# The ternary feed-forward of one transformer layer run as half steps between the pairs of the cross-attention ahead of it

## The chip, the cores and the metric

The kernel runs on one core of one Trainium2 chip. The metric is the device time of one execution in microseconds, from the first to the last instruction with what lies around it; lower is better. Each time given for a kernel is the median of several executions, and the profile is of one execution of its own.

## The reference

Two layers on x (32 batches, 64 tokens, 256 columns) with a context of 1601 keys per batch. Cut to what matters here, in the order in which it is computed:

```
x = x + xattn0(layernorm(x), ctx)       # one head of 256, 1601 keys
x = x + attn0(layernorm(x))             # causal, 64 tokens of a batch
x = x + ffn0(layernorm(x))              # the part that the change moves
x = x + xattn1(layernorm(x), ctx)       # 16 heads
x = x + attn1(layernorm(x))
x = x + moe1(layernorm(x))              # 8 experts, two per token

def ffn0(x):
    h = bit_linear(x, w1)               # 256 -> 1024
    h = silu(depthwise_conv1d(h))       # 3 taps along the 64 tokens, bias
    return bit_linear(h, w2)            # 1024 -> 256

def bit_linear(x, w):
    scale = 127 / clip(max(abs(x), axis=-1), 1e-5)
    xq = round(x * scale) / scale       # a scale per token
    ws = 1 / clip(mean(abs(w)), 1e-5)
    wq = clip(round(w * ws), -1, 1) / ws
    return xq @ wq.T
```

## The kernel before

The kernel is written by hand in five queues (sync, gpsimd, scalar, tensor, vector); each engine runs its own list in order, and semaphores tie them together. There is no planner: the order of the work is the order of the statements.

Phase A holds the first cross-attention and the causal attention. x lies in SBUF as 16 tiles of 128 tokens (two batches each). For every tile (a "pair", `pe_pair_a`, `act_pair_a`, `vec_pair_a`) TensorE multiplies the folded queries with the two batches' contexts (line 1040, four score chunks in PSUM banks 4 to 7), VectorE takes the row maximum over 1601 columns (line 1578), ScalarE the exp (line 738), TensorE transposes the probabilities (line 1049, 13 blocks), VectorE copies them to SBUF (lines 1586 and 1588), TensorE weighs the context rows (line 1060), prepares the next tile's queries, transposes the result and applies the output matrix (line 1077). The causal attention of the tile before runs in between (`transpose_xs`, `project_s`, `scores_s`, `transpose_p_s`, `weigh_s`; `norm_s`, `mask_s`, `add_s` on VectorE). The 14 middle pairs are a hardware loop. SP loads the transposed context of the next pair when the scores are done and the rows of it when the weighted sum is done (lines 370 and 372).

Phase F, the ternary feed-forward, starts when all of x is through phase A. It runs 4 chunks of 512 tokens, one after the other. In each, VectorE normalises and quantises four tiles to bf16 integers, TensorE transposes them and multiplies with the ternary w1 (line 1117, eight blocks of 128 hidden rows), VectorE scales the result by the token's step into a padded buffer (line 1647), POOL computes the centre tap and bias (line 537), VectorE the two side taps (lines 1518 and 1520), ScalarE the silu (line 775). Then VectorE takes the maximum over all 1024 hidden rows of every token (line 1653 across the eight blocks, then over partitions through a transpose), scales (line 1670; POOL takes the odd blocks, line 542) and rounds them (line 1672), TensorE multiplies with the ternary w2 (line 1133) and VectorE adds the product to x (line 1676).

Phase B, the second cross-attention and what follows, waits for all of x (XDONE_F): SP loads w_kv then (line 391). SP's queue between the last scores and that load holds the w_cp loads, two large pad_rows stores to slots_d and a context load. Phase M, the experts, comes last.

The steps of the prediction touch the lines above, `rsqrt` on POOL (lines 495 and 497), and the reload of weights at the start (VectorE rounds w1 and w2, lines 1538 to 1542).

## Time and profile before

| | |
|---|---|
| median of 3 runs | 2910.5 us (2908.04 to 2916.0) |
| the profiled execution | 2910.0 us |
| its span | 2908.3 us |
| TensorE matmul busy | 2535.7 us (87%) |
| VectorE busy | 1727.1 us (59%) |
| ScalarE busy | 1337.5 us (46%) |
| GpSimd busy | 907.7 us (31%) |
| DMA | 283.13 MB, mean 97 GB/s |

The busy times are sums over the whole span and mix phases with different limits. In the rows further down PE is TensorE, DVE is VectorE, ACT is ScalarE, POOL is GpSimd and SPq is the queue of SyncE, from which the loads are issued. Starts are in us from the start of the span. What stands in square brackets behind a row of the timeline is how long the engine had sat idle before it, and what ended that.

### The profile page before, as it was taken

The page shows a single profiled execution, that of the slowest core. Times are in us where ns is not written, and L with a number is a line of the kernel's source. Part 1 is how long each engine was busy: PE and PEld are TensorE (multiplying, and loading weights), DVE is VectorE, ACT ScalarE, POOL GpSimd, SP SyncE. Part 2 cuts the span into 40 slices and gives each one's busy share as a digit, 9 for nine tenths or more (in the row PEclk, how much of TensorE's full clock was granted, in tenths as well). Part 3 has the DMA queues.
Part 4 walks back from the last instruction along what each step waited for, and adds up shares of the span by engine and source line. Part 5 has one row for each costly group of instructions (what it writes and reads, how often), then busy time and mean ns, then how long its engine had stood idle before and what let it go on. Part 6 is the DMA issues. An engine that isn't in the chain of part 4 may idle for free.

```text
span 2908.3 us, 76158 instructions
## 1 busy us (share of the span) xinstructions
PE 2535.7 (87%) x32240; PEld 2148.8 (74%) x32244; DVE 1727.1 (59%) x2970; ACT 1337.5 (46%) x2130; POOL 907.7 (31%) x910
## 2 busy tenths in 40 slices
PE   6999933318999999999999999999999986999997
PEld 3555511117888888888888888888888864999997
DVE  3434367752465675665665665665666664677775
ACT  1211211114555555555555555555555532555554
POOL 1000023344434434434434434434434401111111
PEclk9999956558999999999999999999999986999999
DMA  8878780001101101101101101101101010666664
GB/s 334 324 309 324 288 262 0 0 18 36 46 25 36 39 28 36 39 28 36 39 28 36 39 28 36 39 28 36 39 28 37 28 49 8 209 205 211 212 204 144
DMA packets 60985, 283.13 MB, mean 97 GB/s; under 512 B 4881, under 2 KB 35986, under 8 KB 46098
## 3 DMA queue, kind: packets, MB, share of 16 engines
q1 hardware_dynamic: 52562, 268.73, 25.6%
q0 software_dynamic: 8160, 10.29, 2.2%
q8 instruction: 238, 3.90, 0.5%
q14 instruction: 25, 0.20, 0.0%
HBM read 247.45 MB, written 33.65 MB: 97 GB/s over the span
## 4 chain that ended last, share of the span: by engine, by line
issue 37%; PE 27%; POOL 21%; DVE 7%; DMA 5%; ACT 3%; POOLq 1%; SPq 0%; ACTq 0%; DVEq 0%
POOL k_lo L561 7%; POOL ctx_lo L569 6%; PE PS L1060 3%; PE PS L1040 3%; PE PS L1428 2%; PE PS L1429 2%; PE PS L1430 2%; POOL qbd_lo L574 2%; DMA unit_raw<-in_experts 2%; PE PS L1352 1%; DMA sum_d<-scaled,xg 1%; PE PS L1188 1%; POOL sideB L588 1%; PE PS L1176 1%; DVE mpart L1696 1%
## 5 line engine op out<-in xcount | busy, mean ns | idle before, releaser
L1696 DVE TENSOR_REDUCE mpart<-PS 128x1 f32<-128x802 f32 (+1 forms) x512 | 484.8, 985 | 254.8 <-PE PS L1176 253.3
L869 ACT ACTIVATE probs<-PS 128x1024 f32<-128x1024 f32 (+1 forms) x416 | 413.4, 1025 | 218.6 <-PE PS L1352 218.6
L569 POOL TENSOR_TENSOR ctx_lo<-ctx_raw,ctx_hi 128x801 fp32r<-128x801 f32 x128 | 223.4, 1756 | 360.8 <-ACT ctx_hi L804 352.3
L561 POOL TENSOR_TENSOR k_lo<-probs,k_hi 128x400 fp32r<-128x400 f32 (+1 forms) x256 | 248.9, 972 | 262.8 <-ACT k_hi L792 262.8
L1352 PE MATMUL PS<-qbd_hi,k_hi 64*128 64x256 f32 (+1 forms) x1664 | 314.0, 374 | 0.0
L1176 PE MATMUL PS<-k_hi,qbd_hi 128*128 128x512 f32 (+2 forms) x1024 | 266.2, 361 | 28.6 <-POOL ctx_lo L569 14.1
L791 ACT COPY probs<-PS 128x400 f32<-128x400 f32 (+1 forms) x256 | 126.3, 493 | 243.0 <-PE PS L1156 213.5
L1163 PE MATMUL PS<-wkv_hi,ctx_hi 128*128 128x256 f32 (+1 forms) x832 | 236.5, 284 | 0.0
L1188 PE MATMUL PS<-probs,vals 128*32 128x64 f32 x13312 | 234.7, 221 | 2.0 <-issue 1.8
L1352 PE MATMUL PS<-qbd_hi,k_lo 64*128 64x256 f32 (+1 forms) x1664 | 235.3, 279 | 0.5 <-issue 0.4
L1352 PE MATMUL PS<-qbd_lo,k_hi 64*128 64x256 f32 (+1 forms) x1664 | 234.7, 279 | 0.0
L1165 PE MATMUL PS<-wkv_hi,ctx_lo 128*128 128x256 f32 (+1 forms) x832 | 234.3, 282 | 0.0
L1164 PE MATMUL PS<-wkv_lo,ctx_hi 128*128 128x256 f32 (+1 forms) x832 | 233.5, 281 | 0.0
L1188 PEld LDWEIGHTS PS<-probs,vals 128*32 128x32 f32 x13312 | 197.3, 110 | 42.4 <-issue 25.1
L1176 PEld LDWEIGHTS PS<-k_hi,qbd_hi 128*128 128x128 f32 x1024 | 175.7, 192 | 62.7 <-DVE mpart L1696 41.0
L1428 PE MATMUL PS<-xT_hi,unit_hi 128*128 128x256 f32 x736 | 209.2, 284 | 3.2 <-DVE xT_lo L1936 2.9
L794 ACT COPY vals<-PS 128x512 f32<-128x512 f32 x192 | 112.8, 588 | 214.8 <-PE PS L1165 214.8
L1429 PE MATMUL PS<-xT_lo,unit_hi 128*128 128x256 f32 x736 | 208.9, 284 | 0.0
L1430 PE MATMUL PS<-xT_hi,unit_lo 128*128 128x256 f32 x736 | 208.7, 284 | 0.0
L1154 PE MATMUL PS<-ctx_hi,wkv_hi 128*128 128x400 f32 (+1 forms) x512 | 187.2, 366 | 17.9 <-POOL ctx_lo L569 17.9
L675 POOL DMA_INDIRECT sum_d<-scaled,xg x46 | 75.6, 1643 | 350.7 <-DVE scaled L1967 343.7
L1155 PE MATMUL PS<-ctx_lo,wkv_hi 128*128 128x400 f32 (+1 forms) x512 | 178.6, 349 | 0.0
(321 smaller groups left out, 6229.6 us busy)
## 6 DMA issues: line engine op xcount, KB each, us to landing
unit_raw<-in_experts SPq DMA_DIRECT2D x46, 1536.0 KB, 6.9
ctxN<-in_ctxN SPq DMA_DIRECT2D x16, 3328.0 KB, 10.7
ctxT<-in_ctxT SPq DMA_DIRECT2D x16, 3204.0 KB, 10.5
ctx_raw<-in_ctxT SPq DMA_DIRECT2D x64, 801.0 KB, 4.5
slots_d<-pad_rows SPq DMA_DIRECT2D x2, 9360.0 KB, 44.8
xg<-slots_d SPq DMA_DIRECT2D x23, 260.0 KB, 2.7
x<-in_x SPq DMA_DIRECT2D x1, 2048.0 KB, 9.8
sum_d<-x SPq DMA_DIRECT2D x1, 2048.0 KB, 13.7
```

The source lines that it names most:

```text
L561: g.tensor_tensor(k_lo[:, n, a, c:c + width], k_raw[p % 2][:, 0:width], k_hi[:, n, a, c:c + width].bitcast(F32), ALU.subtract).then_inc(s. ...
L569: g.tensor_tensor(ctx_lo[:, a, cols], ctx_raw[:, cols], ctx_hi[:, a, cols].bitcast(F32), ALU.subtract).then_inc(s.ctx_lo_ready, 1)
L869: act.activation(probs[rows, t % PROBS, :], PS[rows, 1024 * (t % 2):1024 * (t % 2) + 1024], ACT.Exp).then_inc(s.pr_ready, 1)
L1163: pe.matmul(to, ctx_hi[:, k, keys], wkv_hi[:, k, D:2 * D], start=k == 0, stop=False)
L1165: mm = pe.matmul(to, ctx_lo[:, k, keys], wkv_hi[:, k, D:2 * D], start=False, stop=k == KT - 1)
L1176: mm = pe.matmul(at, qbd_hi[:, n, pair // 4, (pair % 4) * P:(pair % 4) * P + P], k_hi[:, n, pair // 4, c:c + width], start=True, stop=True)
L1188: mm = pe.matmul(bank(4, S, slice(32 * j, 32 * j + 32), g * S), vals[rows, n, mine:mine + 32], probs[rows, t % PROBS, at_head(h):at_head(h ...
L1352: mm = pe.matmul(bank(2 * (t % 2) + r, 256, rows, a * 256), keys_part[part, n, a, keys], queries[part, n, a, r * 256:r * 256 + 256], start ...
L1428: pe.matmul(to, hi[:, k, cols], tokens_hi[:, k, :], start=k == 0, stop=False)
L1429: pe.matmul(to, hi[:, k, cols], tokens_lo[:, k, :], start=False, stop=False)
L1430: mm = pe.matmul(to, lo[:, k, cols], tokens_hi[:, k, :], start=False, stop=k == KT - 1)
L1696: v.tensor_reduce(mpart[:, pair, half:half + 1], PS[:, at:at + width], AX, ALU.max).then_inc(s.mx_red, 1)
```

## The change

Phase F as a stage of its own goes. Its work is cut into 8 chunks of 256 tokens, and each chunk into tasks at fixed distances (3 to 18) from its first half step 4f. Half step 2i runs inside pair i of phase A, half step 2i+1 between pairs i and i+1; steps 33 to 46 come after the last pair. Every queue is written out (the loop over pairs too) and calls the tasks by `chunk_at`. POOL keeps the reciprocal roots only: ScalarE computes the centre tap from PSUM, with 1x256 per block, and VectorE both side taps from PSUM. VectorE alone multiplies all 2048 hidden columns of a chunk by the row scale and rounds them, in two instructions. The step of x is multiplied in before the first product instead of after it, so that product runs on float32r in two parts (high and rest), with w1 kept as float32r. Silu is one instruction of 2048 columns, with a dummy exp behind it while phase A lasts. ScalarE takes two of the four copies of the transposed probabilities. The causal attention uses banks 0 and 2, the output product bank 7, and banks 1 and 3 belong to the feed-forward. The last score chunk waits for the normalised tile (`xs_ready`).

The diff, cut to its core:

```diff
-CHUNK = 512
+CHUNK = 256
+HID_BUFS = 3
+GROUPS = HT // 2
+FFN_STEPS = 4 * CHUNKS + 15
+def chunk_at(step, at):
+    f, late = divmod(step - at, 4)
+    return [f] if late == 0 and 0 <= f < CHUNKS else []
-        w1q = sb("w1q", [P, KT, HID], BF16)
+        w1q = sb("w1q", [P, KT, HID], F32R)
 # gpsimd
+            def ffn(at):
+                for _ in chunk_at(at, 3) + chunk_at(at, 5):
+                    rsqrt(mv_f, rstd_f)
...
 # scalar
+            def centre_taps(q):
+                f, m = divmod(q, GROUPS)
+                act.wait_ge(s.h_ps, q + 1)
+                for n in range(2):
+                    j = 2 * m + n
+                    act.activation(hidden_f[:, f % HID_BUFS, j, :], bank(1, CHUNK, at=n * CHUNK), ACT.Identity,
+                                   bias=convb[:, j:j + 1], scale=convw[:, j, 1:2]).then_inc(s.h_mid, 1)
+            def ffn(step):
+                for m in range(GROUPS):
+                    for f in chunk_at(step, 9 + m):
+                        centre_taps(GROUPS * f + m)
+                for f in chunk_at(step, 8):
+                    act.wait_ge(s.xf_ps, f + 1)
+                    act.copy(xsT_hi[:, :, :].rearrange("p k t -> p (k t)"), bank(3)).then_inc(s.xf_hi_ready, 1)
+                for f in chunk_at(step, 17):
+                    act.wait_ge(s.rows_ps, f + 1)
+                    act.copy(rowscale[:, :], bank(3, CHUNK)).then_inc(s.rows_ready, 1)
+                for f in chunk_at(step, 13):
+                    act.wait_ge(s.taps_done, HT * (f + 1))
+                    mine = hidden_f[:, f % HID_BUFS, :, :].rearrange("p j t -> p (j t)")
+                    act.activation(mine, mine, ACT.Silu).then_inc(s.silu_done, 1)
+                    if step < 2 * TILES:
+                        act.activation(reload[:, :], eps[:, :], ACT.Exp)
             # act_pair_a, after the exp and copy_qkv
+                act.wait_ge(s.pT_ps, 4 * i + 2)
+                act.copy(probsAT[:, 4:8, :].rearrange("p t q -> p (t q)"), bank(6)).then_inc(s.pTa_ready, 1)
+                act.wait_ge(s.pT_ps, 4 * i + 4)
+                act.copy(probsAT[0:LAST_KEYS, 12, :], bank(0, P, slice(0, LAST_KEYS))).then_inc(s.pTa_ready, 1)
+                ffn(2 * i)
...
             # its end, after the copy of attT
+                ffn(2 * i + 1)
 # tensor
+            def hidden_group(q):
+                f, m = divmod(q, GROUPS)
+                if q:
+                    pe.wait_ge(s.taps_done, 2 * q)
+                if m == 0:
+                    pe.wait_ge(s.xf_lo_ready, f + 1)
+                for n in range(2):
+                    cols = slice((2 * m + n) * P, (2 * m + n) * P + P)
+                    for a in range(KT):
+                        pe.matmul(bank(1, CHUNK, at=n * CHUNK), w1q[:, a, cols], xsT_hi[:, a, :], start=a == 0, stop=False)
+                        mm = pe.matmul(bank(1, CHUNK, at=n * CHUNK), w1q[:, a, cols], xsT_lo[:, a, :], start=False, stop=a == KT - 1)
+                mm.then_inc(s.h_ps, 1)
+            # ffn(step): groups at 9 to 12, transposes of x at 8, of the maxima at 15,
+            # row scales at 17, second product (16 matmuls) at 18
             # pe_pair_a
                 if not first:
                     transpose_xs()
                     project_s()
+                ffn(2 * i)
                 pe.wait_ge(s.probsA_ready, T["probsA"].up())
...
                 if not first:
                     weigh_s()
+                ffn(2 * i + 1)
                 pe.wait_ge(s.attT_ready, T["attT"].up())
 # vector
+            def side_taps(q):
+                f, m = divmod(q, GROUPS)
+                v.wait_ge(s.h_mid, 2 * (q + 1))
+                # for both blocks the left tap, then for both the right one:
+                    v.scalar_tensor_tensor(acc[:, :, 1:S], h[:, :, 0:S - 1], convw[:, j, 0:1], acc[:, :, 1:S], ALU.mult, ALU.add)\
+                     .then_inc(s.vec_step, 1)
+                v.wait_ge(s.vec_step, T["step"].up(2))
...
+            def hidden_max(f, k):
+                v.wait_ge(s.silu_done, f + 1)
+                v.tensor_reduce(hmax[:, k * P:k * P + P], hidden_f[:, f % HID_BUFS, :, k * P:k * P + P].rearrange("p j t -> p t j"), AX, ALU.max,
+                                apply_absolute_value=True).then_inc(s.hmax_ready, 1)
+            def scale_hidden(f):
+                mine = hidden_f[:, f % HID_BUFS, :, :]
+                v.wait_ge(s.rows_ready, f + 1)
+                stepped(v.tensor_tensor(mine, mine, rowscale[:, None, :].broadcast_to([P, HT, CHUNK]), ALU.mult))
+                v.tensor_scalar(hq[:, :, :], mine, MAGIC, MAGIC, ALU.add, ALU.subtract).then_inc(s.hq_ready, 1)
+            def ffn(step):
+                for f in chunk_at(step, 8):
+                    rest_of_xf(f)
+                for m in range(GROUPS):
+                    for f in chunk_at(step, 9 + m):
+                        side_taps(GROUPS * f + m)
+                for f in chunk_at(step, 17):
+                    scale_hidden(f)
+                for f in chunk_at(step, 18):
+                    add_ffn(f)
+                for f in chunk_at(step, 15):
+                    hidden_steps(f)
+                for k in range(TPC):
+                    for f in chunk_at(step, 3 + 2 * k):
+                        moments_f(TPC * f + k)
+                    for f in chunk_at(step, 13 + k):
+                        hidden_max(f, k)
+                for k in range(TPC):
+                    for f in chunk_at(step, 4 + 2 * k):
+                        quantise_x(TPC * f + k)
             # vec_pair_a
                 if not first:
                     norm_s(x[:, i - 1, :])
+                    ffn(2 * i - 1)
                 v.wait_ge(s.scores_ps, T["scores"].up())
...
                 if not first:
                     mask_s()
+                ffn(2 * i)
                 v.wait_ge(s.probsA_ready, T["probsA"].up())
```

`rest_of_xf` subtracts the high part of the transposed x from PSUM (512 columns). `quantise_x` normalises a tile, takes its row maximum, and scales, rounds and rescales it: four instructions on 256 columns and five on one. `hidden_steps` reduces the transposed maxima (256 columns), has four small instructions and two diagonals of 128 columns. `add_ffn` adds two tiles.

## Rows read from the trace of the kernel before

**Rows 1.** Windows: start:end, us, busy of PE, PEld, DVE, ACT, POOL, clock, DMA, GB/s.
```profile
26.00:366.00 340.00, 306.12 (x2083) 181.95 (x2083) 140.24 (x363) 66.21 (x169) 22.14 (x60) 0.99 0.80 313
378.00:625.00 247.00, 73.66 (x300) 39.39 (x304) 186.20 (x336) 38.99 (x63) 83.70 (x88) 0.57 0.18 57
```

**Rows 2.** Timeline of PE over one pair: start, duration, instruction, count, idle before.
```profile
219.49 5.61 PE L1040 MATMUL PS<-ctxT,big 128*64 128x512 f32 x32
...
226.94 1.13 PE L1016 MATMUL PS<-w_sv,big 128*128 128x256 f32 x4
228.93 1.64 PE L1049 MATMUL PS<-ident,big 128*128 128x128 f32 x13 [0.86 <-ACT big L738]
...
240.53 0.65 PE L1040 MATMUL PS<-ctxT,big 128*64 128x512 f32 x2
```

**Rows 3.** Timeline of DVE over the same pair.
```profile
219.71 0.42 DVE L1599 TENSOR_TENSOR x<-PS,x 128x256 f32 x1 [0.77 <-PE PS L1077]
...
221.97 0.41 DVE L1494 TENSOR_SCALAR big<-x,mv_s,rstd_s 128x256 f32 x1 [0.93 <-POOL rstd_s L497]
225.14 1.82 DVE L1578 TENSOR_REDUCE small<-PS 128x1 f32<-128x1601 f32 x1 [2.77 <-PE PS L1040]
...
229.62 1.89 DVE L1586 COPY big<-PS 128x512 f32<-128x512 f32 x3 [0.46 <-PE PS L1049]
...
236.87 0.48 DVE L1595 TENSOR_SCALAR cat<-PS,small 128x256 f32<-128x256 f32 x1 [4.39 <-PE PS L1060]
...
239.49 0.48 DVE L1570 SCALAR_TENSOR_TENSOR x<-PS,small,x 128x256 f32 x1 [2.08 <-PE PS L1029]
```

**Rows 4.** Timeline of ACT over the same pair.
```profile
225.50 0.37 ACT L718 COPY big<-PS 128x256 f32<-128x256 f32 x1 [7.12 <-PE PS L1006]
227.19 1.60 ACT L738 ACTIVATE big<-PS,small 128x1601 f32<-128x1601 f32 x1 [1.32 <-DVE small L1580]
```

**Rows 5.** Timeline of PE at the end of phase A.
```profile
364.56 1.13 PE L1077 MATMUL PS<-vout,attn_ch 128*128 128x256 f32 x4
368.35 0.44 PE L1006 MATMUL PS<-ident,big 128*128 128x128 f32 x2 [2.66 <-DVE big L1494]
...
370.48 2.07 PE L1016 MATMUL PS<-w_sv,big 128*128 128x256 f32 x4
```

**Rows 6.** Timeline of SP's queue after the last scores.
```profile
351.38 7.97 SPq L377 DMA_DIRECT2D w_cp<-in_w_cp  x16
...
384.66 28.16 SPq L388 DMA_DIRECT2D ctx_raw<-in_ctxT  x1
625.11 0.36 SPq L391 DMA_DIRECT2D probs<-in_w_kv  x1
```

**Rows 7.** Lines by form, one chunk of phase F: busy us, mean ns, then idle before.
```profile
L1653 DVE TENSOR_REDUCE big<-ctxN 128x512 f32<-128x4096 f32 x1 | 7.2, 7171 | 0.7 <-ACT ctxN L775 0.7
...
L1627 DVE TENSOR_REDUCE small<-big 128x1 f32<-128x256 f32 x4 | 1.4, 408 | 0.0
...
L1629 DVE TENSOR_SCALAR small<-small 128x4 f32<-128x4 f32 x1 | 0.2, 169 | 0.0
```

**Rows 8.** Timeline and source of long DVE rows outside phase F.
```profile
634.04 1.22 DVE L1866 TENSOR_TENSOR wkv_lo<-probs,wkv_hi 128x1024 fp32r<-128x1024 f32 x1 [0.97 <-ACT wkv_hi L882]
...
L1542 DVE TENSOR_SCALAR w1q<-work x1: 1227/1227/1227, 29.0 to 29.0; 128x2048 bf16<-128x2048 f32 x1
```

**Rows 9.** Lines by form, ACT in the same chunk of phase F.
```profile
L775 ACT ACTIVATE ctxN<-work 128x512 f32<-128x512 f32 x8 | 5.0, 629 | 13.1 <-DVE work L1520 13.1
...
L775 ACT ACT_TABLE_LOAD x1 | 1.3, 1283 | 0.0
```

**Rows 10.** Timeline of PE, 52 f32r matmuls; the first and the last.
```profile
666.39 0.28 PE L1164 MATMUL PS<-wkv_lo,ctx_hi 128*128 128x256 f32 x1
...
672.41 0.28 PE L1164 MATMUL PS<-wkv_lo,ctx_hi 128*128 128x256 f32 x1
```

**Rows 11.** The chain that ended last, first pair: transposes of the probabilities.
```profile
37.88 3.04 PE PS L1049 x13
```

More of the change, by code:

```diff
@@ L1027, in weigh_s, with added @@
             def weigh_s():
                 pe.wait_ge(s.spT_ready, T["spT"].up())
-                pe.matmul(bank(2, D, at=256), pT_s, v_s, start=True, stop=True).then_inc(s.so_ps, 1)
+                pe.matmul(bank(2, D), pT_s, v_s, start=True, stop=True).then_inc(s.so_ps, 1)
                 T["x_done"].up()
-            def pe_pair_a(first, last):
+            def added(f):
+                return min(2 * (2 * f + 8) + 1, 2 * TILES) + TPC * (f + 1)
+            def hidden_group(q):
[10 more added lines that the diff above has]
+                mm.then_inc(s.h_ps, 1)
@@ L1035, in pe_pair_a @@
+            def pe_pair_a(i):
+                first, last = i == 0, i == TILES - 1
                 pe.wait_ge(s.qk_ready, T["qk"].up())
@@ L1037, in pe_pair_a @@
                 for n, (c, width) in enumerate(KEY_CHUNKS):
+                    if n == len(KEY_CHUNKS) - 1 and not first:
+                        pe.wait_ge(s.xs_ready, i)
                     for k in range(KT):
@@ L1557, in mask_s @@
                 v.wait_ge(s.ss_ps, T["ss"].up())
-                v.tensor_tensor(s_s, bank(3, P), causal[:, :], ALU.add).then_inc(s.vec_step, 1)
+                v.tensor_tensor(s_s, bank(2, P, at=256), causal[:, :], ALU.add).then_inc(s.vec_step, 1)
                 v.wait_ge(s.vec_step, own())
@@ L1569, in add_s, with stepped @@
                 v.wait_ge(s.so_ps, T["so"].up())
-                v.scalar_tensor_tensor(xi, bank(2, D, at=256), small[:, 7:8], xi, ALU.mult, ALU.add).then_inc(s.x_done, 1)
+                v.scalar_tensor_tensor(xi, bank(2, D), small[:, 7:8], xi, ALU.mult, ALU.add).then_inc(s.x_done, 1)
                 T["x_done"].up()
-            def vec_pair_a(before, xi, after):
-                if before is not None:
-                    norm_s(before)
+            def stepped(ins):
+                ins.then_inc(s.vec_step, 1)
+                v.wait_ge(s.vec_step, own())
@@ new lines, in scale_hidden, with add_ffn @@
+            def scale_hidden(f):
[3 more added lines that the diff above has]
+                v.tensor_scalar(hq[:, :, :], mine, MAGIC, MAGIC, ALU.add, ALU.subtract).then_inc(s.hq_ready, 1)
+            def add_ffn(f):
+                v.wait_ge(s.o_ps, f + 1)
+                for k in range(TPC):
+                    xk = x[:, TPC * f + k, :]
+                    v.scalar_tensor_tensor(xk, bank(3, D, at=k * D), h_step[:, k:k + 1], xk, ALU.mult, ALU.add).then_inc(s.x_done, 1)
+                T["x_done"].up(TPC)
@@ L1595, in vec_pair_a @@
                 v.tensor_scalar(att, bank(4, D), small[:, 3:4], None, ALU.mult).then_inc(s.att_ready, 1)
[L1596 to L1597 removed]
+                if not first:
+                    add_s(x[:, i - 1, :])
                 v.wait_ge(s.outA_ps, T["outA"].up())
[L1599 removed]
+                v.tensor_tensor(xi, bank(7, D), xi, ALU.add).then_inc(s.x_done, 1)
                 T["x_done"].up()
[L1602 removed]
+            vec_pair_a(0)
@@ L1603, in _ @@
             v.wait_ge(s.weights_in, WEIGHTS_IN)
-            with v.Fori(1, TILES - 1) as i:
-                enter("A", i, 1)
-                vec_pair_a(tile_of_x(i - 1), tile_of_x(i), tile_of_x(i + 1))
-            leave("A", TILES - 2, 1)
-            vec_pair_a(x[:, TILES - 2, :], x[:, TILES - 1, :], None)
+            for i in range(1, TILES):
+                vec_pair_a(i)
             norm_s(x[:, TILES - 1, :])
+            ffn(2 * TILES - 1)
             mask_s()
+            ffn(2 * TILES)
@@ L1679, in _, with tile_of_x @@
-            leave("F", CHUNKS)
+            for step in range(2 * TILES + 1, FFN_STEPS):
+                ffn(step)
+            v.wait_ge(s.x_done, XDONE_F)
+            def tile_of_x(i):
+                return x[:, bass.ds(i, 1), :].rearrange("p a n -> p (a n)")
             def end_batch(b):
```

367 lines of the change are left out of this document (141 added, 226 removed).

## The prediction

> **What bounds the kernel now.** I read the windows by stage first. [rows 1] give two stages before the second cross-attention: the first cross-attention (26 to 366 us), TensorE busy 306 of 340 us at clock 0.99, and the ternary feed-forward (378 to 625 us), TensorE busy 74 of 247 us, VectorE 186, clock 0.57. The change folds the second stage into the first, so I then read one pair of the first engine by engine. One pair takes 21.04 us from scores to scores [rows 2]. TensorE hardly pauses: its largest wait is the 0.86 us for the softmax. VectorE in the same pair [rows 3] waits 2.77 us for the scores and 4.39 us for the weighted sum; ScalarE waits 7.12 us in one piece [rows 4]. So the pair is TensorE's, and the others have holes in two places: at the seam between pairs, and in the middle behind the softmax.
>
> In [rows 5] stands the last pair: its output matmul ends at 364.56 + 1.13 = 365.69. [rows 6] have SP issuing the w_kv load at 625.11, as soon as the last feed-forward tile is added. These **259.4 us** are what the change replaces; the 2283 us after it run the same code and I leave them as they are. The profiled execution took 2910.0 us (span 2908.3 and 1.7 around it), the median of the runs is 2910.5, so nothing has to be converted. A difference of 0.3% (9 us) is about what a measurement of this kernel can tell.
>
> **The prices of a half step, on VectorE.** A chunk is now 256 tokens (8 chunks) and its work is spread over half steps 4f+3 to 4f+18. Per chunk:
> - taps of one hidden group: four scalar_tensor_tensor on 252 PSUM columns, the 256-column one is 0.48 and overlaps its follower slightly [rows 3]: 1.8 us, four times. The centre tap moves from POOL to ScalarE (two copies' worth of 0.37 [rows 4]).
> - scale and round, 2048 columns: the 1024-column tensor_tensor takes 1.22, so 2048 take 1.22 + 1024 x 1.04 ns = 2.3; the rounding to bf16 of 2048 columns is 1.23 [rows 8]. Together 3.55.
> - maximum over the hidden rows: 7.17 us for 4096 read across rows [rows 7], a quarter each: 1.8, twice. At the rate of the plain reduce of 1601 in 1.82 [rows 3] it would be 1.2.
> - quantise a tile: four operations on 256 columns at up to 0.41 [rows 3, 7], four small ones at 0.17: 2.3, twice. Moments: between the add (ends 220.13) and the wait for POOL (from 221.04) [rows 3]: 0.9, twice.
> - maxima to steps: 0.41, four small ones, two 128-column diagonals at about 0.25: 1.7. Rest of x: a 512-column read of PSUM, 0.7. Adding two tiles: 0.9.
>
> With every fourth half step the same four kinds recur: seam A (steps 17, 9, 13, 5 of four chunks) 1.8 + 3.55 + 1.8 + 0.9 = 8.05; middle A 1.8 + 0.9 + 1.8 + 2.3 = 6.8; seam B 1.8 + 1.7 + 0.9 = 4.4; middle B 0.7 + 1.8 + 2.3 = 4.8. That is 24 us a chunk.
>
> **On TensorE.** f32r matmuls of 256 columns follow each other every (672.41 - 666.39) / 51 = 0.118 us [rows 10]. A hidden group is 8 of them, 1.1 us with its tail; the second product is 16 of bf16, put at the same rate, 1.9; the transposes of x 0.6, those of the maxima 0.44, the row scales 0.55 (a 128-column f32 transpose is 1.64 / 13 [rows 2], a matmul with its diagonal twice that).
>
> **What of it lies on the path.** Two stretches of a pair.
> - From the first score matmul to the first probability transpose: 9.4 us now [rows 2]. VectorE's lane in it: normalised 2.9 us after the start (222.38), then the half step, then maximum, negation and exp, 225.14 to 228.93 = 3.8 [rows 2, 3]. With seam B 2.9 + 4.4 + 3.8 = 11.1, **+1.7**; with seam A 14.75, **+5.3**. TensorE's own lane is 8.6 (end of the v projection, 228.07) plus 1.7 or 3.0 of the middle half step: 10.3 and 11.6, hidden under VectorE's. TensorE then pauses some 3 us for the softmax after seam A.
> - From there to the end of the output matmul: 11.6 us. VectorE has 4.39 of waiting, some 0.9 from two of four copies of the probabilities (three take 1.89 [rows 3], the last is short) that ScalarE takes, and about 1.2 more, since TensorE takes att only after the next queries: 6.5. Middle B (4.8) costs nothing; middle A (6.8) **+0.4**. TensorE does seam work ahead of the output matmul, 1.65 or 1.55, less 0.25 of a wait it covers: **+1.4 and +1.3**. Were this cover gone, 4.8 and 6.8 would come on top in full.
>
> ScalarE: at seam A it has two centre taps, a copy, a table load of 1.28, silu on 2048 columns (512 take 0.63 [rows 9], and 1601 take 1.60 [rows 4], so about 2.0) and the load back with a dummy exp, 1.5: 5.9 us in its hole of 7.12. Off the path; in the middle it has 2 us in 4 of idle time.
>
> Two pairs: 1.7 + 5.3 + 0.4 + 1.4 + 1.3 = 10.1 us, so 26.1 a pair. The pipeline fills slowly: laid out with the same lanes, pairs 1 to 3 cost nothing, the next four 1.1, 1.6, 2.2 and 3.0, then four times 10.1, and the last pair 1.5 more, since it loses a shortening that TensorE had without next queries. **Stage one grows by 7.9 + 40.4 + 1.5 = 50 us.**
>
> **The tail**, half steps 31 to 46 on VectorE after the last output matmul: 4.4 + 4.8 + 8.05 + 6.8 + 3.5 + 2.5 + 7.15 + 4.5 + 3.5 + 1.8 + 5.35 + 2.7 + 1.7 + 0 + 3.55 + 0.9 = 61.2, with 3.1 for the last tile of the causal attention: 64.3. Its waits, as TensorE at the lower clock (0.57 in this stage now [rows 1]; 2.07 / 1.13 times longer [rows 5], with its fixed part a little more) needs 2.1 for a group and 3.6 for the second product: 1.8 around that tile, 2.3 for the transposed x, 4.2 for hidden groups, 5.7 for three second products, 0.9 and 1.6 for maxima and row scales: 16.5. **81 us**.
>
> Added waits: the last score chunk waits for the normalised tile (ready 2.9 us in, wanted after about 5.1), a hidden group for the taps of the one before, always a half step old until the tail; neither holds what is queued behind it. The loop over pairs is written out; the last pair, written out already, shows no issue waits [rows 5], so I cost it at nothing. SP's queue isn't late: from the last scores, w_cp and pads take 384.66 - 351.38 = 33.3 and the ctx_raw issue 28.2 [rows 6], 61 us, and w_kv is asked for at about 104. The context loads of a pair have more time than now. POOL keeps two small operations per tile; its memset after the stage stays behind the same signal.
>
> **Sum:** 2910.0 - 259.4 + 50 + 81 = **2782 us** (2781.6).
>
> **The clock, by row and by rule.** After the pause of 2.66 us and thin work, the v projection ran 2.07 us where a matmul group of the same count and width took 1.13 [rows 5]; 13 transposes at the start took 3.04 [rows 11] against 1.64 [rows 2]. A dense stretch like the pair before such a pause is nowhere in the trace, so a pause of 3 us costs between nothing and a lower clock on the transposes (1.4 us as at the start) and some of the weighted sum behind them, 2 us in all. I take nothing, as work before and behind the pause is dense. The Trainium skill (TensorE: Matmul & The Clock Gate, section HAM oscillation) says that a kernel whose TensorE keeps pausing between short bursts loses its clock at each pause; by it the sum would be 4 x 2 = 8 us more.
>
> **Bounds.** Low: maxima at 1.2, taps 1.5, scaling 3.3, quantise 2.0, TensorE at 2.4 GHz: stage one +38, tail 64, 2910.0 - 259.4 + 102 = 2753. High: groups at 1.9 (lower clock everywhere), scaling 4.6, taps 2.0, quantise 2.8: +73 and 100, 2824.
>
> **Rivals.**
> 1. The pauses of seam A cost the clock each time: four times 2, **2790**. For it: [rows 5]. Against: a burst of over 20 us precedes. Chance 0.17.
> 2. Nothing overlaps, since each queue runs in its order and VectorE's half steps hold up the maximum and att in full: the whole 24 us a chunk lands in the path, stage one +131 (24 x 8 = 192 less the tail's 61) in place of 50: **2863**. The change then doesn't do what it says. Against: the holes of [rows 3]. Chance 0.06.
> 3. Slower than before: once the weave is full (eight pairs), the pauses keep TensorE at 1.2 GHz between them. A pair has 306.12 / 340 x 21.04 = 18.9 us of TensorE work [rows 1] and half of a chunk's 7.9, 22.9; at half clock it costs 22.9 less some 2.7 of pauses, 20.2 more, eight times 162: **2944**. It decides from 128 / 20.2 = 6.3 such pairs on. Against: clock 0.99 with 90% busy [rows 1]; the new busy share is 22.9 / 26.1 = 88%. For it: nothing but the 0.57 of the thin stage. Chance 0.03.
>
> **Numbers.** Forecast 0.74 with its own range 2753 to 2815, rivals 0.17, 0.06, 0.03. The range 2753 to 2824 holds the first two cases nearly whole and leaves out a little over 0.1. Faster by over 0.3%: 0.74 + 0.17 + 0.06 = 0.97, less 0.01 for a mix of rivals 2 and 3 near zero: 0.96; same 0.01; slower 0.03.
>
> **What would show it.** In the profile after: pairs alternating near 24.2 and 28.2 us between output matmuls, with VectorE never waiting for the scores at seam A; TensorE waiting about 3 us for the softmax every second pair at clock 1.0; the last output matmul near 416 us, the w_kv issue near 497; silu of 2048 columns near 2.0 and two table loads a chunk up to chunk 4. Wrong if pairs are even at 21 to 22 (ScalarE and VectorE cheaper), if the clock is below 0.9 in stage one, or if the tail is over 100 us.

## The result, and the profile after it

The changed kernel takes **2774.5 us** (median of 4 runs, 2772.3 to 2778.8) beside 2910.4 us for the kernel before: ratio **0.9532**, 95% interval 0.9514 to 0.9550, so 136 us or 4.7% less. A second set of five runs gave 2774.1 us beside 2907.8, ratio 0.9536 (0.9523 to 0.9550). The forecast was 2782.

The profiled execution took 2772.3 us, its span is 2770.6. TensorE was busy for 91% of it, VectorE 61%, ScalarE 50%, GpSimd 30%. The windows by stage, as in [rows 1], with the same columns; the second stage is now only the tail of the woven feed-forward, from the last output matmul to the w_kv load:

```profile
26.00:406.00 380.00, 343.53 (x2387) 221.52 (x2387) 244.87 (x646) 128.11 (x277) 32.47 (x88) 0.97 0.74 287
406.00:484.00 78.00, 39.80 (x188) 29.05 (x186) 59.68 (x127) 20.54 (x36) 2.21 (x6) 0.69 0.66 202
```

TensorE works in 90% of the first stage, as before, and VectorE in 64% where it was 41%. The timeline of PE, then that of SP's queue, at the end of the stage answer to [rows 5, 6]:

```profile
405.46 1.03 PE L1141 MATMUL PS<-vout,attn_ch 128*128 128x256 f32 x4
```

```profile
384.73 7.30 SPq L388 DMA_DIRECT2D w_cp<-in_w_cp  x16
...
417.90 28.20 SPq L399 DMA_DIRECT2D ctx_raw<-in_ctxT  x1
484.42 0.36 SPq L402 DMA_DIRECT2D probs<-in_w_kv  x1
```

The last output matmul ends at 406.49 (365.69 before: +40.8) and w_kv is issued at 484.42 (625.11 before). So the replaced 259.4 us became 40.8 + 77.9 = **118.7 us**, where the forecast had 50 + 81 = 131. What follows w_kv takes 2770.6 - 484.4 = 2286.2 us, 3.0 more than before the change; in a second trace of the changed kernel it takes 2281.5, 1.7 less than before the change, so the rest is unchanged within what one execution varies. SP is through with its stores and the context load at 446.1, 38 us before w_kv is asked for. For this reason the issue of w_kv is the measure in the experiments below: it leaves out the noise of 2280 us of unchanged code.

The timeline of PE in a long and a short pair, beside [rows 2]:

```profile
226.18 5.61 PE L1098 MATMUL PS<-ctxT,big 128*64 128x512 f32 x32
...
235.55 1.92 PE L1084 MATMUL PS<-w2q,hq 128*128 128x256 bf16 x16
240.20 2.38 PE L1110 MATMUL PS<-ident,big 128*128 128x128 f32 x13 [2.73 <-ACT big L752]
...
243.23 6.36 PE L1123 MATMUL PS<-ctxN,big 128*64 128x256 f32 x52
...
254.20 2.37 PE L1098 MATMUL PS<-ctxT,big 128*64 128x512 f32 x10
...
264.49 1.64 PE L1110 MATMUL PS<-ident,big 128*128 128x128 f32 x13 [0.32 <-ACT big L752]
266.48 5.83 PE L1123 MATMUL PS<-ctxN,big 128*64 128x256 f32 x52
...
277.15 5.60 PE L1098 MATMUL PS<-ctxT,big 128*64 128x512 f32 x32
```

The pairs alternate as forecast: 28.02 us (226.18 to 254.20) and 22.95 (to 277.15), 28.2 and 24.2 expected. The long one pauses 2.73 us for the softmax. What was not in the sum stands right behind the pause: 13 transposes take 2.38 instead of 1.64, and the weighted sum 6.36 instead of 5.83. From the first transpose to the end of the sum it is 243.23 + 6.36 - 240.20 = 9.39 us, in the short pair 7.82. Windows of that stretch, in the columns of [rows 1], have TensorE's granted clock (third number from the end) at its upper level through the pause, lower behind it, and up again before the pair is over:

```profile
237.00:240.00 3.00, 0.47 (x5) 0.17 (x2) 2.00 (x6) 1.54 (x2) 1.16 (x3) 1.00 1.01 424
240.20:244.30 4.10, 4.10 (x21) 3.17 (x23) 2.46 (x7) 2.36 (x7) 0.00 (x0) 0.59 0.30 125
247.00:250.00 3.00, 3.00 (x28) 1.72 (x23) 2.83 (x8) 0.00 (x0) 0.00 (x0) 1.00 0.00 0
```

VectorE at the seam of that long pair, and its second maximum, beside [rows 3]:

```profile
228.44 0.41 DVE L1520 TENSOR_SCALAR big<-x,mv_s,rstd_s 128x256 f32<-128x256 f32 x1 [0.93 <-POOL rstd_s L508]
228.77 0.86 DVE L1613 SCALAR_TENSOR_TENSOR hidden_f<-PS,convw,hidden_f 128x252 f32<-128x252 f32 x2
229.66 0.87 DVE L1619 SCALAR_TENSOR_TENSOR hidden_f<-PS,convw,hidden_f 128x252 f32<-128x252 f32 x2
230.45 2.28 DVE L1645 TENSOR_TENSOR hidden_f<-hidden_f,rowscale 128x2048 f32<-128x2048 f32 x1
232.76 1.23 DVE L1646 TENSOR_SCALAR hq<-hidden_f 128x2048 bf16<-128x2048 f32 x1
233.91 1.95 DVE L1625 TENSOR_REDUCE hmax<-hidden_f 128x128 f32<-128x1024 f32 x1
...
236.45 1.79 DVE L1685 TENSOR_REDUCE small<-PS 128x1 f32<-128x1601 f32 x1
...
246.52 1.93 DVE L1625 TENSOR_REDUCE hmax<-hidden_f 128x128 f32<-128x1024 f32 x1
```

The 2.77 us wait for the scores of [rows 3] is gone: from 228.44 on VectorE runs without a gap up to the maximum over 1601 columns. ScalarE in the same seam, beside [rows 4, 9]:

```profile
226.28 1.28 ACT L743 ACT_TABLE_LOAD   x1
227.57 1.91 ACT L743 ACTIVATE hidden_f<-hidden_f 128x2048 f32<-128x2048 f32 x1
229.50 1.28 ACT L745 ACT_TABLE_LOAD   x1
...
238.46 1.60 ACT L752 ACTIVATE big<-PS,small 128x1601 f32<-128x1601 f32 x1 [5.91 <-DVE small L1687]
```

ScalarE still waits 5.91 us in front of the exp, so silu and both table loads are hidden.

### The profile page after: what moved, and what is told of

Read it like the earlier page. It is cut to its first block, busy times and chain, and to the rows that moved or that the text cites. A ratio compares the mean times of both kernels' runs of the same rounds, so it can differ in the third digit from the quotient of the medians.

```text
span 2770.6 us, 75625 instructions
## 1 busy us (share of the span) xinstructions
PE 2530.7 (91%) x32404; PEld 2171.7 (78%) x32404; DVE 1696.2 (61%) x3035; ACT 1376.4 (50%) x2201; POOL 835.8 (30%) x854
## 4 chain that ended last, share of the span: by engine, by line
PE 57%; DVE 13%; issue 11%; DMA 7%; POOL 6%; ACT 4%; SPq 0%; POOLq 0%; DVEq 0%; ACTq 0%
PE PS L1378 7%; PE PS L1214 6%; PE PS L1202 5%; DVE mpart L1738 3%; PE PS L1123 3%; PE PS L1191 3%; PE PS L1189 3%; PE PS L1190 3%; PE PS L1374 3%; POOL ctx_lo L557 3%; DMA unit_raw<-in_experts 2%; DMA sum_d<-scaled,xg 2%; PE PS L1180 2%; DVE sideB L1727 2%; PE PS L1454 2%
## 5 line engine op out<-in xcount | busy, mean ns | idle before, releaser
L1378 PE MATMUL PS<-qbd_hi,k_lo 64*128 64x256 f32 (+1 forms) x1664 | 234.2, 278 | 0.0
L1378 PE MATMUL PS<-qbd_lo,k_hi 64*128 64x256 f32 (+1 forms) x1664 | 234.2, 278 | 0.0
L1191 PE MATMUL PS<-wkv_hi,ctx_lo 128*128 128x256 f32 (+1 forms) x832 | 234.2, 282 | 0.0
L1214 PEld LDWEIGHTS PS<-probs,vals 128*32 128x32 f32 x13312 | 196.8, 110 | 41.4 <-issue 24.2
## 6 DMA issues: line engine op xcount, KB each, us to landing
ctxN<-in_ctxN SPq DMA_DIRECT2D x16, 3328.0 KB, 11.1
x<-in_x SPq DMA_DIRECT2D x1, 2048.0 KB, 10.4
```

What stands on the lines that cost most here:

```text
L1191: mm = pe.matmul(to, ctx_lo[:, k, keys], wkv_hi[:, k, D:2 * D], start=False, stop=k == KT - 1)
L1214: mm = pe.matmul(bank(4, S, slice(32 * j, 32 * j + 32), g * S), vals[rows, n, mine:mine + 32], probs[rows, t % PROBS, at_head(h):at_head(h ...
L1378: mm = pe.matmul(bank(2 * (t % 2) + r, 256, rows, a * 256), keys_part[part, n, a, keys], queries[part, n, a, r * 256:r * 256 + 256], start ...
```

## The experiments

All were edits of one thing in the changed kernel, unless said otherwise. "Stage" is the end of the last output matmul (406.5 after the change), "tail" what lies from there to the issue of w_kv (77.9). Edits 1 to 7 were timed once each, so for them the trace counts more than the time.

**1. The new form without the overlap.** The half steps are shifted by 30, so that all of them run behind the last pair.

```diff
-FFN_STEPS = 4 * CHUNKS + 15
+LATER = 30
+FFN_STEPS = 4 * CHUNKS + 15 + LATER
-    f, late = divmod(step - at, 4)
+    f, late = divmod(step - LATER - at, 4)
...
-                return min(2 * (2 * f + 8) + 1, 2 * TILES) + TPC * (f + 1)
+                return 2 * TILES + TPC * (f + 1)
```

The second pair of lines is the number of tile additions that a wait counts on, which moves with the order of the work.

> The changed kernel with every task of the feed-forward moved 30 half steps later, so that all of it runs after the last pair, in its new form. If the gain is the overlap: the last output matmul ends near 366 again (pairs of 21.0 us), the feed-forward then takes 228 us (192 of VectorE work and some 33 of waits), w_kv is asked for near 594 instead of 484.4, and the time is near 2882. Of the 137.7 us some 31 would be the new form and 107 the overlap. If the new form itself (wide instructions, no POOL, smaller chunks) is what gained, w_kv comes before 520 and the time is below 2810.

Measured: 2883.4 us beside 2905.6 for the kernel before; w_kv at 599.99, pairs of 21.04 us. The stage ends at 365.80, so the new form alone takes 234.2 us, 6 more than expected, where the old one takes 259.4. Its window, beside the second of [rows 1]:

```profile
378.00:594.00 216.00, 105.11 (x448) 82.77 (x448) 174.68 (x430) 54.86 (x89) 11.81 (x32) 0.56 0.21 65
```

Of the 140.7 us by which w_kv comes earlier, **25.1 are the new form and 115.6 (599.99 - 484.42) the overlap.** VectorE is busy for 175 of 216 us there: a chunk costs it 21 to 22 us, and only where TensorE's pairs leave it idle does that cost nothing.

**2. Scaling and rounding in eight pieces of 256 columns** instead of two instructions of 2048.

```diff
-                stepped(v.tensor_tensor(mine, mine, rowscale[:, None, :].broadcast_to([P, HT, CHUNK]), ALU.mult))
-                v.tensor_scalar(hq[:, :, :], mine, MAGIC, MAGIC, ALU.add, ALU.subtract).then_inc(s.hq_ready, 1)
+                for j in range(HT):
+                    stepped(v.tensor_tensor(mine[:, j, :], mine[:, j, :], rowscale[:, :], ALU.mult))
+                    v.tensor_scalar(hq[:, j, :], mine[:, j, :], MAGIC, MAGIC, ALU.add, ALU.subtract).then_inc(s.hq_ready, 1)
```

> The changed kernel with the hidden rows scaled and rounded in eight pieces of 256 columns instead of two instructions of 2048. If VectorE's half step sets the seam where it scales: a piece takes about 0.44 + 0.29, eight 5.8 instead of 3.5, so the four long pairs go from 28.0 to 30.3, the stage grows by 9 and the tail by 8, w_kv near 501, time near 2789. If TensorE bounds the pairs, the stage stays within 2 us and only the tail grows.

Measured: 2792.1 us, w_kv at 504.30, 19.9 later. The stretch takes 5.3 us (16 instructions of 0.42 and 0.29) instead of 3.5. PE at the same place:

```profile
241.27 3.04 PE L1110 MATMUL PS<-ident,big 128*128 128x128 f32 x13 [4.19 <-ACT big L752]
244.96 6.79 PE L1123 MATMUL PS<-ctxN,big 128*64 128x256 f32 x52
```

1.8 us more of VectorE at the seam made the pause 1.5 us longer in all four long pairs. In this one the slow time behind it grew too, from 9.39 to 10.5 us; in the other three it was 9.2 to 9.4. The long pair went from 28.0 to 30.9 (30.2 and 29.8 in the next two), the short one stayed at 22.95, and the stage ended 9.0 us later for 4 x 1.8 = 7.2 us more on VectorE. So VectorE's half step at seam A is on the path at one to one or more. The tail is 10.9 us longer (88.8): there each chunk's second product waits for the whole stretch, 1.8 us more for each, and up to 4 us may be what runs 9 and 10 show of the tail.

**3. Half of the scaling on GpSimd** (columns 1024 to 2047, in one instruction), as the kernel before shared it.

```diff
+                for f in chunk_at(at, 17):
+                    g.wait_ge(s.rows_ready, f + 1)
+                    far = hidden_f[:, f % HID_BUFS, HT // 2:HT, :]
+                    g.tensor_tensor(far, far, rowscale[:, None, :].broadcast_to([P, HT // 2, CHUNK]), ALU.mult).then_inc(s.odd_scaled, 1)
...
```

> The changed kernel with GpSimd multiplying half of the hidden columns (1024) by the row scale while VectorE does the other half. If GpSimd is as slow beside VectorE as before the change (1.59 us for 512 columns), VectorE waits for it: its part takes 4.0 to 4.3 instead of 3.5, w_kv near 489, time near 2777. If the help counts, 1.1 us less a chunk, w_kv near 476, time near 2764.

Measured: 2777.7 us, w_kv at 493.36, 8.9 later. Long pairs 29.45, 29.95 and 29.50, stage 412.2, tail 81.1. The timeline of POOL, then of DVE:

```profile
227.00 2.37 POOL L523 TENSOR_TENSOR hidden_f<-hidden_f,rowscale 128x1024 f32<-128x1024 f32 x1
```

```profile
227.07 2.45 DVE L1524 TENSOR_SCALAR big<-x,mv_s,rstd_s 128x256 f32<-128x256 f32 x1 [0.93 <-POOL rstd_s L508]
...
231.12 1.22 DVE L1650 TENSOR_TENSOR hidden_f<-hidden_f,rowscale 128x1024 f32<-128x1024 f32 x1
232.37 0.69 DVE L1651 TENSOR_SCALAR hq<-hidden_f 128x1024 bf16<-128x1024 f32 x1
232.98 0.68 DVE L1653 TENSOR_SCALAR hq<-hidden_f 128x1024 bf16<-128x1024 f32 x1
```

VectorE's own part is 1 us shorter, and GpSimd was done before VectorE came to it. Yet VectorE's normalisation, which takes 0.41 us alone, took 2.45 beside GpSimd's 2.37: it ended at 229.52, just behind GpSimd's 229.37. 2.04 lost, 1.0 won; the pause became 3.75 us, 1.0 longer, the transposes behind it 3.04 (from there to the end of the sum 9.2 to 10.5 us in the four long pairs), and the long pairs are 1.4 to 1.9 longer.

**4. The kernel before, with VectorE alone scaling and rounding a whole chunk.** GpSimd's share is removed; 4096 columns in two instructions.

```diff
-                for j in range(HT):
-                    if j % 2:
-                        v.wait_ge(s.odd_scaled, T["odd"].up())
-                    else:
-                        v.tensor_tensor(hs[:, j, :], hs[:, j, :], rowscale, ALU.mult).then_inc(s.vec_step, 1)
...
+                v.tensor_tensor(hs, hs, rowscale[:, None, :].broadcast_to([P, HT, CHUNK]), ALU.mult).then_inc(s.vec_step, 1)
+                v.wait_ge(s.vec_step, own())
+                v.tensor_scalar(hq, hs, MAGIC, MAGIC, ALU.add, ALU.subtract).then_inc(s.hq_ready, 1)
```

> The kernel before with one part of the change alone: VectorE alone scales and rounds, 4096 columns at once, GpSimd takes none. Scaling and rounding of a chunk took 9.7 us (425.56 to 435.26) and should take 4.4 + 2.3 = 6.8, four times 2.9 less: w_kv at 613.3 instead of 625.1, time near 2898. If GpSimd's share was a real help, it grows instead.

Measured: 2896.6 us beside 2905.6; w_kv at 614.75, 10.4 earlier (10.1 of it behind the last output matmul). The timeline of DVE in the second chunk, first of the kernel before, then of this one:

```profile
486.84 0.69 DVE L1670 TENSOR_TENSOR ctxN<-ctxN,big 128x512 f32<-128x512 f32 x1 [2.79 <-ACT big L777]
487.57 2.77 DVE L1672 TENSOR_SCALAR hq_buf<-ctxN 128x512 bf16<-128x512 f32 x2
490.26 1.75 DVE L1670 TENSOR_TENSOR ctxN<-ctxN,big 128x512 f32<-128x512 f32 x1
...
495.06 0.68 DVE L1670 TENSOR_TENSOR ctxN<-ctxN,big 128x512 f32<-128x512 f32 x1
495.77 0.76 DVE L1672 TENSOR_SCALAR hq_buf<-ctxN 128x512 bf16<-128x512 f32 x2
```

```profile
485.06 4.42 DVE L1664 TENSOR_TENSOR ctxN<-ctxN,big 128x4096 f32<-128x4096 f32 x1 [2.78 <-ACT big L775]
489.51 2.29 DVE L1666 TENSOR_SCALAR hq_buf<-ctxN 128x4096 bf16<-128x4096 f32 x1
```

While GpSimd multiplied (from 486.89, four instructions of 6.24 us in all), VectorE's pair of roundings took 2.77 us instead of the 0.76 that it took once GpSimd was through, and its multiply 1.75 instead of 0.68; the multiply at 486.84, which began just ahead of GpSimd's, was not slowed. With VectorE alone the stretch is 6.7 us (485.06 to 491.80) instead of 9.7 (486.84 to 496.53), though VectorE does twice the multiplying. Ten of the 25.1 us of the new form can thus be had by this alone.

**5. The pause filled.** 20 matmuls into a bank that is written afresh by the second product, in front of it, while the pairs run.

```diff
                     pe.wait_ge(s.hq_ready, f + 1)
+                    if step < 2 * TILES:
+                        for _ in range(20):
+                            pe.matmul(bank(3, D), hq[:, 0, 0:P], w2q[:, 0, :], start=True, stop=True)
```

> The changed kernel with 20 matmuls whose result is thrown away ahead of the second product in the four long pairs, 2.4 us of work where TensorE paused 2.73 us. If the pause costs the clock: transposes and weighted sum in those pairs take 7.8 instead of 9.4 us from start to end, the long pairs 26.5 instead of 28.0, w_kv near 478, time near 2766. If the clock falls for another reason (or not at the pause), the long pairs stay at 28.0 and w_kv at 484.

Measured: 2767.9 us in one run, w_kv at 483.91. The pause is down to 0.56 us and the work behind it is at full speed:

```profile
239.86 1.64 PE L1113 MATMUL PS<-ident,big 128*128 128x128 f32 x13 [0.56 <-ACT big L752]
241.84 5.84 PE L1126 MATMUL PS<-ctxN,big 128*64 128x256 f32 x52
```

243.23 + 6.36 - 240.20 = 9.39 became 7.82, in all long pairs: the slow transposes were the pause's doing. The long pair fell only from 28.03 to 27.05 (26.5 expected), since VectorE's middle half step became late: the weighted sum ends at 247.68, and VectorE comes to its result at 249.49.

So the lost clock cost a long pair 1.0 us, not 1.6. And little of that reached the end: the stage ends at 404.49, only 2.0 us earlier, since in its last pair TensorE waited 2.10 us for VectorE and the clock fell behind that wait instead:

```profile
400.00 0.44 PE L1137 MATMUL PS<-ident,cat 128*128 128x128 f32 x2 [2.10 <-DVE cat L1703]
...
402.58 1.91 PE L1144 MATMUL PS<-vout,attn_ch 128*128 128x256 f32 x4
```

The output product took 1.91 us instead of 1.03. The tail took back 1.5 us, so w_kv, expected at 478, came only 0.5 earlier. The rest of the 6.5 us by which this one execution was faster than the median of the changed kernel lies elsewhere.

**6. The maximum by halves.** Three elementwise maxima (1024, 512, 256 columns) in the middle half step, in place of two reduces across rows, one of them at the seam. The absolute value is left out.

```diff
-                v.tensor_reduce(hmax[:, k * P:k * P + P], hidden_f[:, f % HID_BUFS, :, k * P:k * P + P].rearrange("p j t -> p t j"), AX, ALU.max,
-                                apply_absolute_value=True).then_inc(s.hmax_ready, 1)
+                stepped(v.tensor_tensor(tree[:, :, :], mine[:, 0:4, :], mine[:, 4:8, :], ALU.max))
+                stepped(v.tensor_tensor(tree[:, 0:2, :], tree[:, 0:2, :], tree[:, 2:4, :], ALU.max))
+                v.tensor_tensor(hmax[:, :], tree[:, 0, :], tree[:, 1, :], ALU.max).then_inc(s.hmax_ready, 1)
```

> The changed kernel with the maximum over the hidden rows taken by three tensor_tensor maxima (1024, 512 and 256 columns, 2.36 us) in one half step, the middle one, instead of two reduces across rows (1.87 each, one of them at the long seam). It leaves out the absolute value: silu never goes below -0.28, so the result is that of the reference where the largest hidden value of a token is above 0.28. If VectorE's lane sets the long seam: the seam shrinks by 1.9, down to TensorE's own lane, the pause shrinks from 2.7 to about 0.6 and the clock holds, long pairs near 25.3, w_kv near 473, time near 2761. If ScalarE's silu or the scores set it, no more than 1 us a pair is gained.

Measured: 2764.9 us in one run, w_kv at 480.74, long pairs 25.64, short ones 22.94. The timeline of DVE, then of PE:

```profile
241.83 1.22 DVE L1627 TENSOR_TENSOR tree<-hidden_f 128x1024 f32<-128x1024 f32 x1
243.08 0.69 DVE L1628 TENSOR_TENSOR tree<-tree 128x512 f32<-128x512 f32 x1
243.80 0.43 DVE L1629 TENSOR_TENSOR hmax<-tree 128x256 f32<-128x256 f32 x1
```

```profile
236.47 1.64 PE L1111 MATMUL PS<-ident,big 128*128 128x128 f32 x13 [0.86 <-ACT big L753]
```

2.3 us do the work of 3.9, and the seam lost 1.9 of them: the pause is back at 0.86, as before the change, and the clock holds. Stage one ended at 397.4, 9.1 earlier; the tail took 83.4, not 77.9, and gave 5.5 back, so w_kv came 3.7 us earlier and not the 11 expected. What lengthened the tail was open.

**7. Without the dummy exp** that loads ScalarE's table back.

```diff
-                    if step < 2 * TILES:
-                        act.activation(reload[:, :], eps[:, :], ACT.Exp)
```

> The changed kernel without the dummy exp behind silu. If a table load is placed right behind the instruction before it and does not wait for the exp's semaphores, it still lands in the idle time of the seam and nothing changes: w_kv at 484.4 within 0.5. If the load comes only when the exp may start, five pairs get 1.3 us longer, w_kv near 491.

Measured: 2772.6 us in one run. The pairs are 28.03 and 22.94 as before and the stage ends at 406.23, 0.26 earlier. ScalarE loads the table all the same, long before the exp has its operand (wait until 238.5):

```profile
232.58 1.28 ACT L750 ACT_TABLE_LOAD   x1
```

The 0.26 us need not be the edit's. In the last long pair the clock stayed up, behind the same pause:

```profile
393.14 1.64 PE L1108 MATMUL PS<-ident,big 128*128 128x128 f32 x13 [2.73 <-ACT big L750]
```

There the transposes and the sum took 7.82 us, in the other three long pairs 9.4. So a pause of 2.73 us does not always lower the clock.

w_kv was at 487.76, not at 484.4: again a longer tail (81.5), though the tail's code differs in nothing. Runs 9 to 12 go after that, and after the tail of run 6.

**8. Edits 5, 6 and 7 together** (absolute value left out).

> The changed kernel with the tree of maxima, the dummy matmuls and no dummy exp together. With the long seam at TensorE's lane already, the dummy matmuls now lengthen that lane (2.4 us against a pause of 0.6), so the three together should be worse than the tree alone: long pairs near 27, w_kv near 480, time near 2768. If the gains add up, w_kv near 467 and time near 2755.

Measured: 2766.7 us (4 runs), ratio 0.9513 (0.9497 to 0.9529), w_kv at 485.24, 5 later than expected. Long pairs 26.75: slower than with the maxima by halves alone (run 6, the "tree"), as its short pause needs no filling and the 20 matmuls only stand in the way. The tail is 82.9.

**9 and 10. The changed kernel and the tree again**, unaltered, timed five times each.

> The changed kernel once more, unaltered, to see how much of the tail (last output matmul of stage one to the issue of w_kv) belongs to the run and not to the kernel. The tail took 77.9 us in the first trace of it, where TensorE's granted clock stayed at 1.00 up to 420 us, and 81.5 us in the trace without the exp reload, where it fell to 0.67 at 410 us already. If it is TensorE's clock that differs from run to run, the pairs repeat at 28.0 and 22.9 us, the last output matmul ends at 406.5 within 0.5 us, and the tail comes out anywhere from 77.5 to 82. If the tail belongs to the kernel, it repeats at 77.9 within 0.5 us, and the missing reload was what made the other one longer. Time within 0.3% of 2774.5 us.

> The maximum by halves once more (the absolute value is left out, as before), timed in five rounds beside the changed kernel. Pairs 25.64 and 22.94 us, last output matmul at 397.4 within 0.5 us. Tail 83.4 us in its first trace: if the clock's timing sets it, 78 to 84 here; if the place of the maximum does (one half step later), 83 to 84 again. In time 5 to 9 us less than the changed kernel, about 2767 us: 9.1 us less before the last output matmul, 0 to 4 us given back in the tail.

Measured: 2774.1 and 2765.5 us. The stage ends at 406.8 and 397.3, both as before, but for the changed kernel by chance: its first eight pairs were through 1.9 us sooner, and the long pairs took 28.3 to 28.4 us, not the expected 28.0. The clock fell as early as the transposes there, which took 2.7 to 2.8 us (2.38, 2.16 and 1.95 in the first trace), so VectorE's second copy began 2.5 us after the first transpose instead of 2.2, and its result of the weighted sum came 0.3 us later too. From the first transpose to the end of the sum it is 9.39 to 9.45 us, as in the first trace.

The tail of the changed kernel is now **81.9** us (488.68 - 406.82) where it was 77.9; that of the tree is 83.4 again. So the tail isn't a property of the kernel alone. Windows from 410 to 420 us in three traces, each with the clock as third number from the end; first the changed kernel:

```profile
410.00:420.00 10.00, 6.64 (x41) 5.23 (x41) 8.46 (x32) 4.43 (x12) 0.74 (x2) 1.00 1.09 336
```

the same kernel again:

```profile
410.00:420.00 10.00, 7.77 (x30) 5.93 (x29) 5.84 (x22) 3.26 (x9) 0.74 (x2) 0.67 1.09 335
```

and the kernel without the dummy exp:

```profile
410.00:420.00 10.00, 8.19 (x31) 6.34 (x32) 6.04 (x23) 2.89 (x8) 0.74 (x2) 0.67 1.09 336
```

In the first the granted clock stays at its upper level (2.4 GHz) for some ten microseconds more, VectorE gets through 32 instructions in the window instead of 22. It begins to scale the first chunk 15.1 us into the tail instead of 18.4, and that lead of 3.3 us is 3.9 at the end. In the other two it falls as soon as the pause of 2.66 us behind the last pair is over. Over the whole tail VectorE's busy time is the same, 59.7 of 78 us and 59.4 of 82 (next fence): only its waits differ, 18.3 and 22.6. The tree's 5.5 us of lost gain were thus mostly this: beside the second trace its tail is 1.5 longer, not 5.5.

**11 and 12. The tail filled**, for the changed kernel and for the tree (absolute value left out in the second).

```diff
                     for f in chunk_at(step, 9 + m):
                         hidden_group(GROUPS * f + m)
+                if step > 2 * TILES:
+                    for _ in range(12):
+                        pe.matmul(bank(6, D), w2q[:, 0, 0:P], w2q[:, 0, :], start=True, stop=True)
```

> The changed kernel with 12 extra 256-column matmuls behind each hidden group of the tail, into a bank that nobody reads there. If the low clock is what stretches the tail: its granted clock rises from 0.65 to over 0.9, the 16 output matmuls of a chunk take 1.9 instead of 3.6 us (four chunks), a hidden group of 8 takes 1.1 instead of 1.8 us, and the tail falls from 77.9 to 68 to 73 us; the time falls by 5 to 10 us. If the clock stays low all the same, each block of extra matmuls costs up to 2.6 us where VectorE's wait for the group is next, and the tail does not fall or grows by up to 8 us. If VectorE's own chain sets the tail (the rival), it stays at 77 to 79 us whatever the clock. Stage one up to the last output matmul is untouched: 406.5 us.

> The maximum by halves (absolute value left out) and the extra matmuls of the tail together. If both theories hold, the two savings add: last output matmul at 397.4, tail 70 to 76, w_kv issued at 467 to 473 us, time 2753 to 2760 us. If the tail is bound by VectorE's chain, w_kv is issued at 477 to 481 us and the time is that of the tree alone.

Measured: 2772.1 us (4 runs, 0.9531, 0.9516 to 0.9545) and 2763.7 us (4 runs, 0.9505, 0.9490 to 0.9520). The tails take 79.8 and 79.6 us. The tail's window of the changed kernel's second trace, then with the extra matmuls:

```profile
406.00:488.00 82.00, 44.59 (x189) 33.25 (x187) 59.37 (x126) 20.63 (x36) 2.21 (x6) 0.60 0.61 189
```

```profile
406.00:486.00 80.00, 51.29 (x353) 41.06 (x353) 60.46 (x128) 20.11 (x34) 2.21 (x6) 0.89 0.64 195
```

The clock rose from 0.60 to 0.89, but the tail fell by 2 us, not by 5 to 10, and even these 2 us aren't shown to be the edit's. In this trace the clock stayed up behind the last pair, as in the first trace of the changed kernel, and VectorE begins to scale the first chunk at the same 15.1 us, before the extra matmuls have made any difference. Beside that trace (77.9) the filled tail is 1.9 us longer. For the tree, 1.5 of the 3.8 us that its tail lost were won before its first extra matmul.

The extra matmuls use up part of what they win (12 take 1.5 us at the upper level and up to 2.8 at the lower), and mostly the tail is VectorE's: 60 of 80 us whatever the clock. The rival in that expectation was nearer. In time the changed kernel with and without the filling can't be told apart (2774.1 and 2772.1), nor can the tree (2765.5 and 2763.7). The tree is 8.7 us faster than the changed kernel (2765.5 against 2774.1, intervals 0.9496 to 0.9522 and 0.9523 to 0.9550). Neither form of the tree computes the absolute value, so a kernel that is to keep it would need another operation in that place; none was tried.

## Why the prediction was right, and which terms were off

**What bounds it.** Right. TensorE set the pair, VectorE's and ScalarE's holes took the work, and run 1 splits the gain into form (25.1) and overlap (115.6). Rival 2 (no overlap) is out by that number.

**Prices.** Scale and round 2.28 + 1.23 = 3.5 (3.55 forecast); a maximum 1.93 to 1.95 (1.8, a quarter of [rows 7]; twice a chunk); taps 1.7 (1.8); quantising a tile 2.2 (2.3); silu with its loads 4.7 of ScalarE's time, hidden. All within the bounds.

**The long pair: 28.2 forecast, 28.0 measured, but for other reasons.** Up to the transposes it took 14.0 us (226.18 to 240.20) against 14.75, from there 14.0 against 13.3. The second part holds the step that failed: "I take nothing, as work before and behind the pause is dense". The lower clock behind the pause made transposes and sum 1.6 us longer (9.39 against 7.82 in run 5, where the pause is filled), and the pair 1.0 us (28.03 against 27.05); without it the second part would be 13.0, a little under the forecast. The last pair lost 0.3 us by it (beside run 7, where the clock held). That is 3.2 us for the four pauses in the first trace. In the second, where the pairs were 28.3 to 28.4 and the last one 1.5 us longer than in run 7, it is 5.5. So rival 1's mechanism was at work at 0.4 to 0.7 of its 8 us, hidden in the total by terms sized too high: that 28.2 met 28.0 is luck. The Trainium skill (TensorE: Matmul & The Clock Gate, section HAM oscillation) had spoken for such a loss, and the rows agree with its direction. But its case is a kernel whose bursts are shorter than its waits and each start at the low clock; here the clock fell behind pauses of 2.73 us in dense work, and over the stage it stood at 0.97.

**The short pair: 24.2 forecast, 22.95 measured.** The lane of 11.1 to the first transpose was 10.3 (254.20 to 264.49), since steps, moments and taps were 0.1 to 0.2 cheaper each, and the taps began 2.6 us after the scores instead of 2.9, for they overlap the normalisation. From there to the end the pair grew by 1.1 instead of 1.4. At the start of the ninth pair the stage was 4.8 us late (203.23 - 198.45, the latter 219.49 less one pair of 21.04). Of these, 0.7 were there before any woven work, and the filling cost 4.1 instead of 7.9 (0.6, 0.6, 0.9 and 1.9 for four pairs). The eight pairs behind it cost 36.0 instead of 41.9. Together 40.8 instead of 50: **the mis-sized term is VectorE's lane in the short pairs and in the filling.**

**The tail: 81 forecast, 77.9 and 81.9 measured.** VectorE's work was 59.5 instead of 64.3, its waits 18.3 and 22.6 instead of 16.5. The estimate sat inside a spread that comes from when TensorE's clock falls, and it did so by luck in part: the work was put 5 us too high and the waits 2 to 6 us too low.

**SP's queue** was named as safe, 61 us of issues in about 104, so with 43 us of margin; it had 38. **Rival 3** (the stage at 1.2 GHz) did not happen: 0.97.

## What to carry to other kernels

Before weaving one stage into another, list each engine's holes per period of the host stage and lay the guest's work out in order, seam by seam: only what exceeds a hole costs time, and then it costs at least one to one, and more where the pause it makes lets TensorE's clock fall. An elementwise operation on SBUF data that VectorE shares with GpSimd should be tried on VectorE alone, in one wide instruction: here it was faster both before and after the change. When two versions differ by a few microseconds, take the point where they rejoin in the trace, and trace one of them twice before explaining the difference.

## What the runs showed of the hardware

- An elementwise tensor-tensor instruction on GpSimd holds up VectorE's own that begins after it: 0.41 us became 2.45 beside a GpSimd instruction of 2.37 (run 3), two roundings of 0.76 became 2.77 and a multiply of 0.68 became 1.75 in the kernel before (run 4). A multiply that began 0.05 us before GpSimd's took its usual 0.69 (run 4).
- A pause of 2.73 us between dense matmuls slowed what came behind it by 1.6 us, in 15 of the 16 long pairs of four traces (the changed kernel twice, runs 7 and 11); in one of run 7 the same pause cost nothing. A wait of 2.10 us lowered the clock in the last pair of run 5 and not in that of run 7. Pauses of 0.86 (run 6) and 0.56 us (run 5) never did.
- In thin work behind the last pair, the same code in the same kernel kept the upper clock for ten microseconds longer in one execution than in another, which moved the end of the stage by 4 us.
- A table load of ScalarE doesn't wait for the operands of the activation that needs it: it started as soon as the instruction before was done, 6 us before the exp (run 7). A dummy activation to bring it forward won nothing here, where ScalarE was idle ahead of the exp anyway.
- A maximum across rows (tensor_reduce over a rearranged view) costs 1.9 us for 1024 elements, so 1.9 ns each; three elementwise maxima over 1792 columns take 2.3 us for twice the data, without the absolute value.
